# Row maxima of an attention turned and loaded in two parts (in the first batch four), and its score blocks spread over the attention before and its own first steps

## The chip, the cores and the metric

One core of one Trainium2 chip runs the kernel. The metric is the device time of one execution in microseconds; the median of three is given.

## The reference

A transformer block with conditioning, on 8 batches of 512 tokens with 256 features, 16 heads of 16 features. Cut to what matters:

```
c6 = silu(c) @ Wc + bc                         # six shifts, scales and gates per batch
xm = ln(x) * (1 + sc_msa) + sh_msa
q, k, v = xm @ Wq + bq, xm @ Wk + bk, xm @ Wv + bv     # (8, 512, 16 heads, 16)
w = softmax(einsum('bqhc,bkhc->bhqk', q / 16, k))
y = einsum('bhqk,bkhc->bqhc', w, v)
x = x + g_msa * (y @ Wo + bo)
h = gelu((ln(x) * (1 + sc_mlp) + sh_mlp) @ W1 + b1)
x = x + g_mlp * (h @ W2 + b2)
```

## The kernel before

The softmax subtracts the true row maximum, so the scores are computed twice. A **score block** is one matmul (line 598): 128 queries of one head against its 512 keys, into one of two score banks (6 and 7). DVE takes its row maximum into `mx` (`row_max`, line 899). There are 16 heads x 4 query tiles = 64 blocks a batch. A block may be issued once the block two before it has had its maximum taken (`max_done`).

When the maxima are there, TensorE **turns** them (`turn_maxima`, line 608: transposes of `mx` into a bank), DVE writes them as two bf16 rows per head, a high and a low part (`maxima_rows`, lines 922 and 924, into `mrow`), and SP loads these into rows 96 and 97 of the q stack (`load_maxima`, line 294). The k stack has -1 there, so that the second, **transposed scores** (line 628, 98 rows) come out with the maximum subtracted, and ACT applies the exponential (line 500). The q and k stacks themselves hold the parts of q and k, and are filled by four large loads a batch, from a DRAM scratch (line 322).

The work is a pipeline written out by hand. `step(i)` holds, in this order: the attention of batch i (sixteen steps `s`; in each the transposed scores of four heads for one key tile in two pairs, then the product with V of the step before, `pv`, line 620); the turning of the normalised x of batch i+2 and of batch i-1; q, k and v of batch i+2; the MLP of batch i-1 (`up` and `down` products for j = 0 to 7); the output projection of batch i (`wo_products`), in whose middle stand the first transposed scores of batch i+1 (`first_transposed`); and at last DVE's `residual` of batch i (lines 1014 and 1017). Steps 2 to 5 are a loop; the others are written out, and in steps -2 and -1 (`early`) there is no attention. The score blocks of batch i+1 are strewn through `step(i)`: `C_BLOCKS` says how many in each step of the attention, `TURN_BLOCKS`, `QK_BLOCKS`, `V_BLOCKS`, `UP_BLOCKS`, `DOWN_BLOCKS` how many at the places after it. In an attention step, `between` puts the first block behind the first pair of transposed scores, the second behind the second pair, the others behind `pv`.

Each engine runs its own list in order. Batch 0 is different already: only the blocks of heads 0 to 7 and eight more are done before its attention, the other 24 stand in its first six steps (`OLD_BLOCKS`), and their maxima are turned after step 5 and awaited at step 8.

DVE also has the layer norms inside the attention, in pieces (`ln2`, `ln1`: 0 to 3 statistics, 4 the variance, 5 to 8 the normalisation of a tile).

Of the kernel before, what the change touches and what calls it, by code (L numbers as in the profile page):

```python
# [53 lines left out]
assert sum(map(sum, (C_BLOCKS, TURN_BLOCKS, QK_BLOCKS, V_BLOCKS, UP_BLOCKS, DOWN_BLOCKS))) == NH * TT  # L54
# [6 lines left out]
assert HALF + EXTRA + sum(OLD_BLOCKS) == NH * TT and OLD_TURN < STEPS // 2  # L61
# [6 lines left out]
def dit_block(nc, x, c, Wc, bc, Wq, bq, Wk, bk, Wv, bv, Wo, bo, W1, b1, W2, b2, out,  # L68
              c6_scr, parts_scr, y_scr, r_scr):
    with ExitStack() as ctx:  # L70
# [97 lines left out]
        half_turned, half_rows, half_loaded = sem("half_turned"), sem("half_rows"), sem("half_loaded")  # L168
# [65 lines left out]

        def c_blocks(i, s):

            return (OLD_BLOCKS[s], NEW_BLOCKS[s]) if isinstance(i, int) and i == 0 else (0, C_BLOCKS[s])

        def tail_blocks(i):

            new = NEW_BLOCKS if isinstance(i, int) and i == 0 else C_BLOCKS
            return NH * TT - sum(map(sum, (new, TURN_BLOCKS, QK_BLOCKS, V_BLOCKS)))
# [8 lines left out]
        def _(sp):  # L251
# [24 lines left out]
            def step(i, par):  # L276
# [14 lines left out]
                def load_maxima(stack, first, last, loaded):  # L291

                    for n in range(2):
                        sp.dma_start(stack[MROW + n:MROW + n + 1, first:last, :], mrow[0:last - first, n, :]).then_inc(loaded, 16)

                if runs(i, 0) and not later(i, 0, 1):
                    sp.wait_ge(mrow_done, 2)
                    load_maxima(qst[par], NH // 2, NH, m_loaded)
                if runs(i, 0):


                    for g in range(NG):
# [50 lines left out]
                if early(i) and runs(i, 1):  # L353
                    sp.wait_ge(half_rows, 2)
                    load_maxima(qst[1 - par], 0, NH // 2, half_loaded)
                elif runs(i, 1):
                    sp.wait_ge(mrow_done, 2 * i + 4)
                    load_maxima(qst[1 - par], 0, NH, m_loaded)
# [189 lines left out]
        def _(pe):  # L548
# [36 lines left out]
            def scores(i, par, blocks, banks=(6, 7)):  # L585

                for _ in range(blocks if runs(i, 1) else 0):
# [7 lines left out]
                    if n == 0:  # L595
                        if later(i, 1, 1):
                            pe.wait_ge(mrow_done, 2 * (i + 1))
# [3 lines left out]
            def turn_maxima(i, first=0, last=NH, turned=mt_done, bank=6):  # L601

                if runs(i, 1):
                    pe.wait_ge(max_done, 64 * (i + 1) + TT * last)
                    if bank == 4:
                        pe.wait_ge(vaug_done, 4)
                    for t in range(TT):
                        m = pe.transpose(ps[0:last - first, bank, t * P:(t + 1) * P], mx[:, t, first:last], ident[:])
                    m.then_inc(turned, 1)
# [22 lines left out]
            def first_transposed(b, par):  # L632

                if later(b, 0, 1):
                    pe.wait_ge(m_loaded, 32 * (b + 1))
                else:
                    pe.wait_ge(half_loaded, 32)
                pe.wait_ge(part_l, 4 * (b + 2) if runs(b, 1) else 4 * NB)
                if later(b, 0, 2):
                    pe.wait_ge(o_gated, b - 1)  # L640
                for p in range(2):
                    transposed_scores(b, par, 0, p)

            def step(i, par):
                has_b, has_c, has_a, has_mlp = runs(i, 1), runs(i, 0), runs(i, 2), runs(i, -1)
                others = (lambda n: 0) if early(i) else (lambda n: n)
                if has_c:
# [4 lines left out]
                    for s in range(STEPS):  # L652
# [7 lines left out]
                        if s == STEPS // 2 and not later(i, 0, 1):  # L660
                            pe.wait_ge(m_loaded, 32)
                        for p in range(2):
# [3 lines left out]
                            if later(i, 0, 1):  # L666
# [6 lines left out]
                        if s == OLD_TURN and not later(i, 0, 1):  # L673
                            turn_maxima(i - 1, NH // 2, NH)
# [66 lines left out]
                if has_mlp:  # L741
# [51 lines left out]
                elif early(i):  # L793
                    scores(i, par, HALF + 2, (6, 7, 0, 1))
                    turn_maxima(i, 0, NH // 2, half_turned, 4)
                    scores(i, par, EXTRA - 2)
                else:
                    scores(i, par, tail_blocks(i))
                    turn_maxima(i)
# [10 lines left out]
        def _(dve):  # L810
# [77 lines left out]
            def row_max(i, blocks, banks=(6, 7)):  # L888
# [3 lines left out]
                for _ in range(blocks):  # L892
                    n = block_at[0]
                    block_at[0] = (n + 1) % (NH * TT)
                    if n == 0 and later(i, 1, 1):
                        dve.wait_ge(mt_done, i + 1)
# [13 lines left out]
            def maxima_rows(i, heads=NH, turned=mt_done, done=mrow_done, bank=6):  # L910

                if not runs(i, 1):
                    return
                if turned is mt_done:
                    dve.wait_ge(mt_done, i + 2)
                    if later(i, 1, 1):
                        dve.wait_ge(m_loaded, 32 * (i + 1))
                    else:
                        dve.wait_ge(half_loaded, 32)
                else:  # L920
                    dve.wait_ge(turned, 1)
                dve.tensor_copy(mrow[0:heads, 0, :], ps[0:heads, bank, :]).then_inc(done, 1)
                dve.wait_ge(done, 2 * (i + 1) + 1)
                dve.tensor_tensor(mrow[0:heads, 1, :], ps[0:heads, bank, :], mrow[0:heads, 0, :], ALU.subtract).then_inc(done, 1)

            def step(i, par):
# [3 lines left out]
                ln2 = {2: (0, 1), 3: (2, 3), 4: (4,), 7: (5, 6), 8: (7, 8)}  # L930
                ln1 = {5: (0, 1), 6: (2, 3), 9: (4,), 12: (5, 6), 13: (7, 8)}
                for s in range(STEPS):
# [13 lines left out]
                    if s == OLD_TURN and has_c and not later(i, 0, 1):  # L946
                        maxima_rows(i - 1, NH // 2)
# [71 lines left out]
                if has_mlp:  # L1019
                    b = i - 1  # L1020
                    row_max(i, UP_BLOCKS[0])
                    for j in range(JT):
# [10 lines left out]
                        if j == JT - 1:  # L1033
                            maxima_rows(i)
# [21 lines left out]
                else:  # L1056
                    if early(i):
                        row_max(i, HALF + 2, (6, 7, 0, 1))
                        maxima_rows(i, NH // 2, half_turned, half_rows, 4)
                        row_max(i, EXTRA - 2)  # L1060
                    else:
                        row_max(i, tail_blocks(i))
                        maxima_rows(i)
# [39 lines left out]
```

## Time and profile before

| | |
|---|---|
| median of three runs | 781.13 us (777.75 to 783.33) |
| the profiled execution | 775.7 us, span 773.8 us |
| TensorE, matmuls | 707.6 us, 91% of the span |
| DVE | 582.3 us, 75% |
| ACT | 384.3 us, 50% |
| GpSimd | 222.3 us, 29% |
| row maxima on DVE (line 899) | 512, 335.4 us, 685 ns each |
| score blocks on TensorE (line 598) | 512 |
| exponentials on ACT (line 500) | 256, 247.9 us, 1022 ns each |
| mean granted clock of TensorE | 0.951 of full speed |

Busy matmul time is modelled and rows overlap, so 91% doesn't say that TensorE runs at its peak. Times within the run are microseconds from the start of the span.

### The profile page before, as it was taken

To read this page: it belongs to the slowest core of one execution; us is meant where nothing else is said; L and a number is where in the kernel's file an instruction comes from. 1 tells how busy PE (TensorE), PEld (TensorE's weight loads), DVE (VectorE), ACT (ScalarE), POOL (GpSimd) and SP (SyncE) were. 2 spreads that over 40 slices of the span, in tenths; PEclk is the share of its full clock that TensorE was granted. 3 is DMA by queue.
4 is the path that set the end of the run, shared out by engine and by line. 5 is a ranking of instruction groups with operands and counts; after the bars stand their busy time and mean duration, and the time that the engine had idled before them with its cause. 6 is when DMAs were issued, how large, how long until landed. Compare 5 with 4: busy or idle time off the path is not lost.

```text
span 773.8 us, 11775 instructions
## 1 busy us (share of the span) xinstructions
PE 707.6 (91%) x3967; PEld 382.9 (49%) x3967; DVE 582.3 (75%) x1015; ACT 384.3 (50%) x462; POOL 222.3 (29%) x163
## 2 busy tenths in 40 slices
PE   4678989769999999999999899999999998998986
PEld 1551222432268425772378225862478225812976
DVE  5769688859886898789887798789886976721463
ACT  0430556217752676347642775257633773298221
POOL 5245001200334031511253032512162022230444
PEclk9785799959999999999999999999999999999998
DMA  8489100681039302860067303840076102021110
GB/s 290 138 253 289 62 21 22 223 203 55 28 136 261 99 28 73 257 165 34 31 218 176 112 15 121 247 141 28 30 243 166 59 27 72 3 82 45 56 35 27
DMA packets 59558, 88.45 MB, mean 114 GB/s; under 512 B 6214, under 2 KB 47708, under 8 KB 56428
## 3 DMA queue, kind: packets, MB, share of 16 engines
q1 hardware_dynamic: 59500, 87.69, 37.0%
q8 instruction: 35, 0.57, 0.3%
q14 instruction: 23, 0.19, 0.1%
HBM read 49.35 MB, written 38.06 MB: 113 GB/s over the span
## 4 chain that ended last, share of the span: by engine, by line
issue 34%; PE 32%; DVE 14%; POOL 11%; DMA 5%; ACT 3%; SPq 1%; POOLq 0%; DVEq 0%; ACTq 0%
DVE mx L899 7%; PE ps L620 7%; PE ps L598 7%; PE ps L628 6%; PE ps L552 5%; POOL hl L445 4%; PE ps L759 3%; POOL prob L438 2%; PE ps L763 2%; DMA qst<-mrow 2%; ACT prob L500 1%; DMA kst<-parts_scratch 1%; POOL x L418 1%; POOL xd L431 1%; POOL zl L397 1%
## 5 line engine op out<-in xcount | busy, mean ns | idle before, releaser
L899 DVE TENSOR_REDUCE mx<-ps 128x1 f32<-128x512 f32 x512 | 335.4, 685 | 62.6 <-PE ps L598 56.4
L500 ACT ACTIVATE prob<-ps 128x1024 f32<-128x1024 f32 x256 | 247.9, 1022 | 156.5 <-PE ps L628 156.2
L598 PE MATMUL ps<-kst,qst 96*128 96x512 bf16 x512 | 196.2, 405 | 24.9 <-DVE mx L899 19.0
L628 PE MATMUL ps<-qst,kst 98*128 98x512 bf16 x512 | 150.4, 385 | 4.0 <-DMA qst<-mrow 2.4
L598 PEld LDWEIGHTS ps<-kst,qst 96*128 96x128 bf16 x512 | 45.5, 98 | 191.5 <-DVE mx L899 165.8
L620 PE MATMUL ps<-prob,vaug 128*32 128x512 f32 x1024 | 137.6, 609 | 0.5 <-ACT prob L500 0.3
L445 POOL TENSOR_TENSOR hl<-z,hh 128x512 fp32r<-128x512 f32 x64 | 82.3, 1287 | 137.3 <-DVE hh L1028 137.3
L539 ACT ACTIVATE z<-ps,bias_t 128x512 f32<-128x512 f32 x64 | 44.1, 689 | 134.5 <-PE ps L763 127.1
L393 POOL TENSOR_TENSOR rstd<-vare,mhalf 128x4 f32<-128x4 f32 x16 | 16.4, 1022 | 249.6 <-DVE vare L839 249.6
L628 PEld LDWEIGHTS ps<-qst,kst 98*128 98x128 bf16 x512 | 46.9, 99 | 70.1 <-ACT prob L500 26.6
L438 POOL TENSOR_TENSOR prob<-prob 128x512 bf16<-128x512 f32 x32 | 37.4, 1167 | 139.7 <-DVE prob L973 139.7
L552 PE MATMUL ps<-w_hi,hh 128*128 128x256 f32 x256 | 73.6, 288 | 0.3 <-POOL hl L445 0.3
L552 PE MATMUL ps<-w_hi,hl 128*128 128x256 f32 x256 | 72.0, 281 | 0.0
L552 PE MATMUL ps<-w_lo,hh 128*128 128x256 f32 x256 | 71.9, 281 | 0.0
L1028 DVE CAST hh<-z 128x512 fp32r<-128x512 f32 x64 | 37.0, 580 | 35.8 <-ACT z L539 35.8
L759 PE MATMUL ps<-zh,w_hi 128*128 128x512 f32 x128 | 60.5, 472 | 2.0 <-DVE zh L904 2.0
L759 PE MATMUL ps<-zh,w_lo 128*128 128x512 f32 x128 | 51.5, 402 | 0.0
L552 PEld LDWEIGHTS ps<-w_hi,hh 128*128 128x128 f32 x256 | 48.2, 188 | 2.9 <-POOL hl L445 0.7
L552 PEld LDWEIGHTS ps<-w_lo,hh 128*128 128x128 f32 x256 | 48.2, 188 | 1.8
L552 PEld LDWEIGHTS ps<-w_hi,hl 128*128 128x128 f32 x256 | 48.2, 188 | 0.0
L620 PEld LDWEIGHTS ps<-prob,vaug 128*32 128x32 f32 x1024 | 20.4, 108 | 46.1 <-issue 41.9
L478 ACT ACTIVATE z<-ps,mod 128x512 f32<-128x512 f32 x30 | 21.7, 774 | 39.9 <-DVE bias_t L883 18.5
(106 smaller groups left out, 854.4 us busy)
## 6 DMA issues: line engine op xcount, KB each, us to landing
parts_scratch<-prob SPq DMA_DIRECT2D x32, 384.0 KB, 2.9
qst<-parts_scratch SPq DMA_DIRECT2D x16, 768.0 KB, 9.1
kst<-parts_scratch SPq DMA_DIRECT2D x16, 768.0 KB, 14.0
parts_scratch<-prob SPq DMA_DIRECT2D x32, 256.0 KB, 3.1
y_scratch<-rb SPq DMA_DIRECT2D x32, 256.0 KB, 2.0
xa<-in_x_dram SPq DMA_DIRECT2D x8, 512.0 KB, 4.4
parts_scratch<-prob SPq DMA_DIRECT2D x32, 128.0 KB, 2.9
xd<-in_x_dram SPq DMA_DIRECT2D x8, 512.0 KB, 3.5
```

The lines of the kernel that those rows point to most:

```text
L438: pool.tensor_tensor(parts[:, j, PART_AT[j // 2][2], :], rest[:, j % 2, :], parts[:, j, 1, :], ALU.subtract).then_inc(part_l, 1)
L445: pool.tensor_tensor(hl[:, j % HR, :], hb[:, j % HB, :], hh[:, j % HR, :].bitcast(F32), ALU.subtract).then_inc(hl_done, 1)
L478: act.activation(z_of(n, b)[:, k, :], ps[:, banks + k, :], ACT.Identity, bias=mod[:, 2 * shift + k, bass.ds(b, 1)], scale=mod[:, 2 * scale ...
L500: act.activation(prob[:, s % 2, 2 * p:2 * p + 2, :], ps[:, 2 * p:2 * p + 2, :], ACT.Exp, scale=1.0 / DH).then_inc(exp_done, 1)
L539: act.activation(hb[:, j % HB, :], ps[:, 4 + j % 2, :], ACT.Gelu, bias=b1_t[:, j:j + 1]).then_inc(gelu_done, 1)
L552: m = pe.matmul(out_, a, b, start=start and n == 0, stop=stop and n == 2, skip_group_check=True)
L598: pe.matmul(ps[:, banks[n % len(banks)], :], qst[1 - par][0:MROW, h, t * P:(t + 1) * P], kst[1 - par][0:MROW, h, :], start=True, stop=True ...
L620: m = pe.matmul(ps[32 * q:32 * q + 32, 4 + g % 2, :], vaug[par][:, kt, G * g + q, :], prob[:, s % 2, q, :], start=kt == 0, stop=kt == TT - ...
L628: m = pe.matmul(ps[:, q, :], kst[par][0:KROWS, G * g + q, kt * P:(kt + 1) * P], qst[par][0:KROWS, G * g + q, :], start=True, stop=True)
L759: pe.matmul(ps[:, 4 + j % 2, :], w1[n][:, k, f], zh_of(1, b)[:, k, :], start=k == 0 and n == 0, stop=False)
L899: dve.tensor_reduce(mx[:, t, h:h + 1], ps[:, banks[n % len(banks)], :], AXX, ALU.max).then_inc(max_done, 1)
L1028: dve.tensor_copy(hh[:, j % HR, :], hb[:, j % HB, :]).then_inc(hh_done, 1)
```

## The change

Every batch now does what batch 0 did, and batch 0 does it by quarters. Before an attention 40 of its 64 blocks are done (batch 0: 24); the others stand in its first six steps, four in each (batch 0: ten steps), and the blocks of the next batch only behind them: two in each of steps 6 to 14, three in step 15 (batch 0: four in each of steps 10 to 15). The maxima of heads 0 to 7 are turned after the first `down` product of the MLP in place of the sixth, those of heads 8 to 15 after step 5 of the attention itself, and awaited at step 8. In batch 0 heads 0 to 3 are turned before the attention, the others after steps 1, 5 and 9, and awaited at steps 4, 8 and 12. The 19 blocks outside the attention are dealt out otherwise: `UP_BLOCKS` 5 in place of 3, `DOWN_BLOCKS` 8 in place of 10. The layer norm's pieces move to later steps. The semaphores of the halves fall away; `mt_done`, `mrow_done` and `m_loaded` now count turns.

```
-C_BLOCKS = (1, 0) + (3,) * (STEPS - 4) + (4, 4)
+HALF, EXTRA = NH * TT // 2, 8
+QUARTER = NH * TT // 4
+OLD_BLOCKS = (4,) * 6 + (0,) * (STEPS - 6)
+NEW_BLOCKS = (0,) * 6 + (2,) * (STEPS - 7) + (3,)
 TURN_BLOCKS, QK_BLOCKS, V_BLOCKS = (1, 1), (0, 1, 0, 1), (0, 1, 0, 1)
-UP_BLOCKS, DOWN_BLOCKS = (1, 1, 1), (2, 2, 2, 2, 2, 0, 0, 0)
-HALF, EXTRA = NH * TT // 2, 8
-OLD_BLOCKS = (4,) * 6 + (0,) * (STEPS - 6)
-NEW_BLOCKS = (0,) * 6 + (4,) * (STEPS - 6)
-OLD_TURN = 5
+UP_BLOCKS, DOWN_BLOCKS = (1, 2, 2), (0, 0, 2, 2, 2, 2, 0, 0)
+DOWN_TURN = 0
+FIRST_OLD = (4,) * 10 + (0,) * (STEPS - 10)
+FIRST_NEW = (0,) * 10 + (4,) * (STEPS - 10)
+TURNS, FIRST_TURNS = {5: 8}, {1: 4, 5: 8, 9: 12}
...
+        def heads_of(b, head):
+            return head + (NH // 4 if first(b) else NH // 2)
+        def turn_no(b, head):
+            return head // 4 + 1 if first(b) else 2 * b + 3 + head // 8
...
                     for g in range(NG):
                         sp.wait_ge(y_evac, NG * i + g + 1)
                         sp.dma_start(y_scr[...], ysb[:, g % 2, :]).then_inc(y_written[g % 2], 16)
+                        if g == 0:
+                            load_maxima(i, qst[par], 8)
+                        if g == 1 and first(i):
+                            load_maxima(i, qst[par], 12)
...
+                    if t == 0 and h in (8, 12) and first(i + 1):
+                        pe.wait_ge(mrow_done, 2 * turn_no(i + 1, h - 4))
+                    elif t == 0 and h == 8:
+                        pe.wait_ge(mrow_done, 2 * turn_no(i + 1, 0))
+                    elif n == 0 and later(i, 1, 1):
+                        pe.wait_ge(mrow_done, 2 * (turn_no(i + 1, 0) - 1))
...
-                        if s == STEPS // 2 and not later(i, 0, 1):
-                            pe.wait_ge(m_loaded, 32)
+                        if s == STEPS // 2 or s and s % TT == 0 and first(i):
+                            pe.wait_ge(m_loaded, 32 * turn_no(i, s))
...
-                        if s == OLD_TURN and not later(i, 0, 1):
-                            turn_maxima(i - 1, NH // 2, NH)
+                        if s in c_turns(i):
+                            turn_maxima(i, c_turns(i)[s])
...
-                        if j == 5:
-                            turn_maxima(i)
+                        if j == DOWN_TURN:
+                            turn_maxima(i + 1, 0)
...
-                    scores(i, par, HALF + 2, (6, 7, 0, 1))
-                    turn_maxima(i, 0, NH // 2, half_turned, 4)
+                    scores(i, par, QUARTER + 2, (6, 7, 0, 1))
+                    turn_maxima(i + 1, 0, 4)
                     scores(i, par, EXTRA - 2)
...
-                ln2 = {2: (0, 1), 3: (2, 3), 4: (4,), 7: (5, 6), 8: (7, 8)}
-                ln1 = {5: (0, 1), 6: (2, 3), 9: (4,), 12: (5, 6), 13: (7, 8)}
+                ln2 = {5: (0, 1), 6: (2, 3), 7: (4,), 9: (5, 6), 10: (7, 8)}
+                ln1 = {7: (0,), 8: (1, 2), 9: (3,), 10: (4,), 12: (5, 6), 13: (7, 8)}
...
-                        if j == JT - 1:
-                            maxima_rows(i)
+                        if j == DOWN_TURN + 2:
+                            maxima_rows(i + 1, 0)
```

## Rows read from the trace of the kernel before

**Rows 1.** windows of batch 5's attention and of the stage after it

```profile
512.20:554.00 41.80, 41.53 (x239) 12.72 (x239) 37.27 (x75) 32.49 (x35) 8.16 (x6) 1.00 0.20 64
554.00:597.00 43.00, 41.11 (x256) 33.82 (x254) 34.26 (x52) 15.48 (x23) 17.27 (x13) 1.00 0.61 180
```

**Rows 2.** table of waits, TensorE: us, times, longest

```profile
PE ps L628 <- DMA qst<-mrow: 2.4, 3, 1.9
```

**Rows 3.** timeline, TensorE, a step with three blocks: start, us, instruction

```profile
539.90 0.39 PE L598 MATMUL ps<-kst,qst 96*128 96x512 bf16 x1
540.13 0.60 PE L628 MATMUL ps<-qst,kst 98*128 98x512 bf16 x2
...
542.75 0.60 PE L628 MATMUL ps<-qst,kst 98*128 98x512 bf16 x2
```

**Rows 4.** timeline, TensorE, batch 7, steps without blocks

```profile
679.75 1.04 PE L628 MATMUL ps<-qst,kst 98*128 98x512 bf16 x4
...
696.56 1.04 PE L628 MATMUL ps<-qst,kst 98*128 98x512 bf16 x4
```

**Rows 5.** timeline, batch 0, a step with four blocks

```profile
93.58 2.58 DVE L899 TENSOR_REDUCE mx<-ps 128x1 f32<-128x512 f32 x4 [0.51 <-PE ps L598]
93.59 1.03 PE L628 MATMUL ps<-qst,kst 98*128 98x512 bf16 x4
...
96.68 1.03 PE L628 MATMUL ps<-qst,kst 98*128 98x512 bf16 x4
```

**Rows 6.** timeline, the seam before batch 5, and the end of its attention

```profile
512.15 1.04 PE L628 MATMUL ps<-qst,kst 98*128 98x512 bf16 x4
...
513.98 0.39 PE L598 MATMUL ps<-kst,qst 96*128 96x512 bf16 x1
...
514.20 1.27 PE L628 MATMUL ps<-qst,kst 98*128 98x512 bf16 x4
...
515.43 1.22 DVE L1017 TENSOR_TENSOR x<-x,xd 128x1024 f32<-128x1024 f32 x1
...
516.57 1.52 DVE L899 TENSOR_REDUCE mx<-ps 128x1 f32<-128x512 f32 x2
...
553.97 1.04 PE L580 MATMUL ps<-ident,xa 128*128 128x128 f32 x8
```

**Rows 7.** timeline, batch 0, the turn after step 5

```profile
98.57 0.42 DVE L828 BATCH_NORM_STATS2 stats<-xa 128x6 f32<-128x256 f32 x1
...
101.60 1.03 PE L628 MATMUL ps<-qst,kst 98*128 98x512 bf16 x4
...
102.51 0.68 DVE L924 TENSOR_TENSOR mrow<-ps,mrow 8x512 bf16<-8x512 f32 x1
...
105.72 1.03 PE L628 MATMUL ps<-qst,kst 98*128 98x512 bf16 x4
```

**Rows 8.** chain that ended last, before batch 0: start, us, what

```profile
53.18 20.42 DVE mx L899 x34
...
74.93 0.78 SPq L294
...
75.75 1.81 DMA qst<-mrow
...
78.32 1.86 PE ps L628 x4
```

**Rows 9.** DMA issues from 65.2 to 65.3: KB, us to landing

```profile
kst<-parts_scratch SPq DMA_DIRECT2D x1, 768.0 KB, 12.7
```

**Rows 10.** chain, then timeline, before batch 1

```profile
163.41 7.20 DMA qst<-mrow
...
170.65 1.04 PE L628 MATMUL ps<-qst,kst 98*128 98x512 bf16 x4 [1.87 <-DMA qst<-mrow]
```

**Rows 11.** windows, PEclk the granted clock

```profile
646.70:650.10 3.40, 3.40 (x10) 2.31 (x9) 1.60 (x4) 0.69 (x1) 0.39 (x1) 0.50 0.29 90
425.60:429.90 4.30, 2.13 (x13) 1.52 (x14) 2.62 (x3) 1.94 (x2) 0.00 (x0) 1.00 0.71 228
```

More of the change, by code:

```diff
@@ L233, in x1_of, with first, c_turns @@
             return xa if final(b) else x1
+        def first(b):
+            return isinstance(b, int) and b == 0
         def c_blocks(i, s):
[L237 to L242, printed above, removed]
+            return (FIRST_OLD[s], FIRST_NEW[s]) if first(i) else (OLD_BLOCKS[s], NEW_BLOCKS[s])
+        def c_turns(i):
+            return FIRST_TURNS if first(i) else TURNS
+        def heads_of(b, head):
+            return head + (NH // 4 if first(b) else NH // 2)
+        def turn_no(b, head):
+            return head // 4 + 1 if first(b) else 2 * b + 3 + head // 8
         def early(i):
@@ L289, in step, with load_maxima @@
                     sp.dma_start(gm[:], c6_scr[bass.ds(i - 1, 1), G2 * H:(G2 + 1) * H].broadcast_to([P, H])).then_inc(gm_loaded, 16)
-                def load_maxima(stack, first, last, loaded):
+                def load_maxima(b, stack, head):
+                    last = heads_of(b, head)
+                    sp.wait_ge(mrow_done, 2 * turn_no(b, head))
                     for n in range(2):
[L294 to L298, printed above, removed]
+                        sp.dma_start(stack[MROW + n:MROW + n + 1, head:last, :], mrow[0:last - head, n, :]).then_inc(m_loaded, 16)
                 if runs(i, 0):
+                    if first(i):
+                        load_maxima(i, qst[par], 4)
                     for g in range(NG):
@@ L352, in step @@
                     load_stack(i + 2, 1, 1)
[L353 to L358, printed above, removed]
+                if runs(i, 1):
+                    load_maxima(i + 1, qst[1 - par], 0)
                 if runs(i, -1):
@@ L594, in scores, with turn_maxima @@
                         pe.wait_ge(stack_loaded[h // 8], 32 * (i + 2))
[L595 to L597 removed]
+                    if t == 0 and h in (8, 12) and first(i + 1):
[4 more added lines that the diff above has]
+                        pe.wait_ge(mrow_done, 2 * (turn_no(i + 1, 0) - 1))
                     pe.matmul(ps[:, banks[n % len(banks)], :], qst[1 - par][0:MROW, h, t * P:(t + 1) * P], kst[1 - par][0:MROW, h, :],
                               start=True, stop=True).then_inc(s_done, 1)
[L601 to L604 removed]
+            def turn_maxima(b, head, bank=6):
+                if runs(b, 0):
+                    last = heads_of(b, head)
+                    pe.wait_ge(max_done, 64 * b + TT * last)
                     if bank == 4:
@@ L607, in turn_maxima @@
                     for t in range(TT):
-                        m = pe.transpose(ps[0:last - first, bank, t * P:(t + 1) * P], mx[:, t, first:last], ident[:])
-                    m.then_inc(turned, 1)
+                        m = pe.transpose(ps[0:last - head, bank, t * P:(t + 1) * P], mx[:, t, head:last], ident[:])
+                    m.then_inc(mt_done, 1)
             def pv(b, par, s):
@@ L665, in step @@
                                 transposed_scores(i, par, s, p)
-                            if later(i, 0, 1):
+                            if not first(i):
                                 between(p, p + 1)
@@ L908, in z_lo, with maxima_rows @@
                 dve.tensor_tensor(zl_of(n, b)[:], z_of(n, b)[:], zh_of(n, b)[:].bitcast(F32), ALU.subtract).then_inc(zl_done[n], 1)
-            def maxima_rows(i, heads=NH, turned=mt_done, done=mrow_done, bank=6):
-                if not runs(i, 1):
+            def maxima_rows(b, head, bank=6):
+                if not runs(b, 0):
                     return
[L914 to L924, printed above, removed]
+                heads, turn = heads_of(b, head) - head, turn_no(b, head)
+                dve.wait_ge(mt_done, turn)
+                if not first(b) or head:
+                    dve.wait_ge(m_loaded, 32 * (turn - 1))
+                dve.tensor_copy(mrow[0:heads, 0, :], ps[0:heads, bank, :]).then_inc(mrow_done, 1)
+                dve.wait_ge(mrow_done, 2 * (turn - 1) + 1)
+                dve.tensor_tensor(mrow[0:heads, 1, :], ps[0:heads, bank, :], mrow[0:heads, 0, :], ALU.subtract).then_inc(mrow_done, 1)
             def step(i, par):
@@ L945, in step @@
                                     norm_piece(0, i + 2, xa, k)
-                    if s == OLD_TURN and has_c and not later(i, 0, 1):
-                        maxima_rows(i - 1, NH // 2)
+                    if has_c and s in c_turns(i):
+                        maxima_rows(i, c_turns(i)[s])
                 row_max(i, others(TURN_BLOCKS[0]))
```

27 lines of the change are left out of this document (13 added, 14 removed).

## The prediction

> **What bounds the kernel now.** I began with the page's busy times, in the table above: TensorE's matmuls fill 91% of the span. The windows of one loop iteration then split it in two. The attention, 512.2 to 554.0, has TensorE busy for 41.53 of 41.80 us, with DVE at 37.27 and ACT at 32.49; the projections and the MLP, 554.0 to 597.0, have it busy for 41.11 of 43.00 [rows 1]. So in the loop TensorE's own queue sets the end, and a change that makes TensorE wait costs its full length. The table of waits says how much the wait for the maxima rows (the one that a half-sized load could shorten) costs now: 2.4 us in three places over the whole run, 1.9 of it in one [rows 2].
>
> The timeline gives a price per attention step. A step has 4 transposed scores, 8 matmuls with V and some score blocks. With three blocks it lasts 542.75 - 540.13 = 2.62 us, and one block delays the next matmul by 540.13 - 539.90 = 0.23 [rows 3]. With no blocks, in the last batch, eight steps take 696.56 - 679.75 = 16.81, so 2.10 each [rows 4]: there ACT's two exponentials set the pace. With four blocks, in the first batch, a step takes 96.68 - 93.59 = 3.09, more than 2.62 + 0.23 = 2.85, and the DVE row says why: four maxima take 2.58 and then DVE is idle 0.51 for the next block [rows 5]. There are only two score banks, so blocks must wait for maxima and maxima for blocks. Four blocks are over the knee, three are not.
>
> **The change in the loop (batches 1 to 6).** The number of blocks inside an attention stays 45 (before 1, 0, twelve times 3, 4, 4; after six times 4, nine times 2, 3), and outside it stays 19. Nothing is saved there; what changes is the order.
>
> - Step 0 has four blocks in place of one. In the trace, DVE does the two residual operations at this seam (lines 1014 and 1017), the second from 515.43 for 1.22 us, and only then its first maximum, at 516.57 (ends overlap the next start a little); the only block of this step was issued at 513.98, long before, and step 1 could begin at 514.20 [rows 6]. After the change blocks 1 and 2 fill both banks at about 514.0 and 514.2; block 3 needs the first maximum, 516.57 + 0.65 = 517.2, block 4 the second, 517.9, and step 1 starts at about 518.2. So step 0 lasts 518.2 - 512.15 = 6.05 in place of 2.05: +4.0. Queued behind the waiting block are all of step 1's transposed scores, and behind them ACT. This is the largest term.
> - Step 1: the V matmuls of step 0 waited for the residual before (it had no block); they no longer do, but it has four blocks. I walk the two-bank handshake through it and get 2.8.
> - Steps 2 to 4: four blocks, 3.09 each, 9.27.
> - Step 5: four blocks and the turn of heads 8 to 15. The first batch did just this: step 5 ran 96.68 to 101.60, 4.92 [rows 5, 7]; TensorE waits for the last maximum, then turns. DVE also did two statistics there, 0.42 each, and will again [rows 7].
> - Step 6: in the first batch 101.60 to 105.72, 4.12, because the next block uses the bank that DVE reads until 102.51 + 0.68 = 103.19 [rows 7]. After, it has two blocks, the first placed between the two pairs of transposed scores. It holds the second pair until about 1.6 after the start; then 0.23 + 0.43 + 0.23 + 1.0 follow. 3.6.
> - Steps 7 to 14: two blocks. No row shows such a step. Bounds: 2.10 (ACT's pace, none) and 2.62 (three). As TensorE is full at three, I take one block off: 2.62 - 0.22 = 2.40; 19.2 for eight.
> - Step 15: three blocks, 2.62.
>
> Sum: 6.05 + 2.8 + 9.27 + 4.92 + 3.6 + 19.2 + 2.62 = 48.5. Before, the same attention ran from 512.15 to 553.97 [rows 6], 41.8. That is +6.6 each, +40 for six. The load of the turned rows is off the path here: the rows are ready 1.6 after step 6 begins, the two issues are 0.8 apart and the second took 1.81 to land before batch 0 [rows 8], some 4.3 in all, and step 8 begins 6.0 after step 6. The norm pieces that move from steps 2 to 8 to steps 5 to 10 go at nothing: steps 7 to 10 have two blocks, so DVE has about 1 us free in each; should that cover go, each piece costs 0.4.
>
> **The last attention (batch 7)** had no blocks and gets 24. Step 0 +4.0, step 1 2.8 - 2.10 = +0.7, steps 2 to 4 3 x 0.99 = +3.0, step 5 4.92 - 2.10 = +2.8; steps 6 and 7 stay at 2.10, so step 8 may find the rows not yet landed, +0.3. Together +10.8.
>
> **The first attention (batch 0)** has 64 blocks as before, in sixteen steps of four, but turns three times instead of once. The turn at step 5 cost 4.92 - 3.09 = 1.8 and 4.12 - 3.09 = 1.0 more, 2.8 in all, some 0.8 of it the statistics on DVE. Two more without these are 2 x 2.0 = 4.0. The turn after step 1 falls where the granted clock is 0.50, +0.5. So +4.5, bounds 2 and 7.
>
> **The two places where blocks are saved.** Before batch 0 sixteen blocks fewer stand ahead of the turn. DVE did the 34 in 20.42 us, 0.60 each, so the rows would be ready 9.6 us earlier than the load at 74.93, at about 65.3 [rows 8]. But this load follows four stack loads of 768 KB in the same queue; the last, issued at 65.2, took 12.7 us to land, so until 77.9 [rows 9]; the rows landed at 75.75 + 1.81 = 77.56 and the first transposed scores began at 78.32 [rows 8]. The new rows' load, a smaller one, would sit behind the same loads and land no earlier than about 77.5. That a small load sits behind the stack loads is shown at the end of the next stage: ready to go at 163.41, it took 7.20 to land, and TensorE, which had sat idle 1.87 for it, went on at 170.65 [rows 10]. So 9.6 us of work are taken from a chain that ends just level with another, and I take a gain of 78.32 - 77.5 = 0.8; likewise 0.3 for the eight blocks fewer in the stage before batch 1. The trace's bounds for both are 0 and 9.6 + 8 x 0.6 = 14.4. In the Trainium skill, "DMA: Bandwidth & Descriptors", section "Queues, rings and completion order", each DMA engine consumes descriptors in ring order, but a DMA on fewer engines may complete before an earlier one on all of them. The trace agrees: 77.56 is 0.3 before the last stack load's end. By that rule a load of four heads on few engines could land somewhat earlier still, and the sum would fall by perhaps another microsecond; each engine still has its share of the stack loads ahead of it.
>
> **The MLP stage.** The turn comes after the first down product instead of the sixth, with the same four transposes and the same two DVE operations; the up products have two more blocks, the down products two fewer. TensorE may wait a few tenths for the last maximum; the wait for the rows at the seam (2.4 less the 1.9 above, so 0.5) goes. I count -0.3 for the whole run.
>
> **Sum** on the profiled execution: 775.7 + 40 + 10.8 + 4.5 - 0.8 - 0.3 - 0.3 = 829.6. The profiled execution is 5.4 under the median of the runs, 781.1, so I add 54 to the median: 835.
>
> **The rivals.**
>
> 1. *The seam wait is hidden* (15%). If DVE could take the first maxima between the residual operations, or ACT's backlog of exponentials covered TensorE's wait, the seven times 4.0 would go: 835 - 28 = 807. Against: DVE runs in order, and the first maximum stands after the second operation in the rows [rows 6], and a step 0 that lasts 6.05 is longer than the four exponentials ACT has in hand (2.10 a pair, by its pace in the last batch).
> 2. *The clock falls* (15%). TensorE's granted clock is 0.50, the lower of its levels 1.2 and 2.4 GHz, for 3.4 us from 646.70, after a stretch with little matmul work. Against: at 425.6 to 429.9 it was busy for 2.13 of 4.30 and kept 1.00 [rows 11]. The new seam has about 2.4 of 6.05. If it fell there in each attention, 3.4 us would run at half speed: +1.7, seven times, 12: 847. The Trainium skill, "TensorE: Matmul & The Clock Gate", section "Part 1: The HAM clock gate", says that idleness takes the clock to the lower level and activity releases it; the rows agree in kind and leave the seam open.
> 3. *Faster* (5%). The stages before batch 0 and before batch 1 are worth their 14.4, the blocks cost TensorE the same wherever they stand, and the last attention pays only six steps at 2.85 - 2.10, 4.5. Then 781 - 14.4 + 4.5 = 771. It needs the small loads to overtake the stack loads (for it: they begin to move while those are in flight) and both handshake and turn to cost nothing, and it decides if the first transposed scores start before 75.
> 4. *No difference* (4%): the same neutrality in the loop, with the loads in order: 781 + 4.5, within 1%. A per cent is about what a measurement of this kernel can tell from no change.
>
> The forecast has 60%; 1% is left for more than 855. The range takes in the first two rivals and the unknown costs. With two-block steps at 2.62 the six attentions cost 11 more, 846; with them at 2.10 and four-block steps at 2.85, 20 less, 815. So 806 to 853.
>
> **What would show it.** In the changed trace: first transposed scores at 78 and batch 1's at about 174 or 175 (its stage unchanged, the attention before it longer); each loop attention near 48.5; at each seam one pause of TensorE of some 3 us ahead of a score block, released by a maximum; DVE nearly idle from 68 to 78; far more waits of score blocks for maxima; two-block steps at 2.40. The prediction is wrong if the loads overtake, if step 1 starts within 3 us of the first transposed scores, or if the two-block steps run at ACT's pace.

## The result and the profile after

The changed kernel takes 858.42 us (854.82 to 858.74, four runs) against 780.52 us for the kernel before (777.75 to 783.33, four runs): ratio 1.0985, 95% interval 1.0958 to 1.1012. Slower as forecast, but by 78 us and not by 54; it lies 5 us above the range. The profiled execution has a span of 855.8 us, so 82 more than before.

The page of the changed kernel: the span, the engines (busy us, share, instructions) and the granted clock in 40 slices.

```profile
span 855.8 us, 11928 instructions
...
PE 735.5 (86%) x4003; PEld 388.7 (45%) x4003; DVE 592.8 (69%) x1033; ACT 386.0 (45%) x462; POOL 222.2 (26%) x163
...
PEclk9785999669999899999999899997999999989999
```

The same clock row of the kernel before:

```profile
PEclk9785799959999999999999999999999999999998
```

TensorE's share falls from the 91% of the table above to 86% although it has 28 us more busy time, and the clock row, nines throughout the loop in the kernel before, now has eights and a seven there; the mean granted clock fell from 0.951 to 0.920. (A matmul counts as busy for longer at the lower clock, so part of those 28 us is the clock itself.)

The seam ahead of batch 5, in the timeline (start, us, instruction, idle before it and its releaser); the rows of before are [rows 6].

```profile
561.79 1.04 PE L649 MATMUL ps<-qst,kst 98*128 98x512 bf16 x4
...
563.62 0.61 PE L618 MATMUL ps<-kst,qst 96*128 96x512 bf16 x2
...
565.08 1.22 DVE L1032 TENSOR_TENSOR x<-x,xd 128x1024 f32<-128x1024 f32 x1
566.22 3.76 DVE L918 TENSOR_REDUCE mx<-ps 128x1 f32<-128x512 f32 x6
...
566.96 0.39 PE L618 MATMUL ps<-kst,qst 96*128 96x512 bf16 x1 [2.73 <-DVE mx L918]
...
567.78 0.60 PE L649 MATMUL ps<-qst,kst 98*128 98x512 bf16 x2
...
570.62 0.60 PE L649 MATMUL ps<-qst,kst 98*128 98x512 bf16 x2
```

The first two score blocks go out at 563.62, DVE finishes the residual at 566.30, and block 3 follows its first maximum at 566.96, after TensorE has been idle for 2.73. From the first transposed scores to step 1 it is 567.78 - 561.79 = 5.99; the forecast was 6.05. Step 1 lasts 570.62 - 567.78 = 2.84 (forecast 2.8).

The turn after step 5 of the same attention, TensorE alone; before, batch 0 had it [rows 7].

```profile
584.53 0.60 PE L629 MATMUL ps<-ident,mx 128*8 128x128 f32 x4 [1.17 <-DVE mx L918]
584.97 0.60 PE L649 MATMUL ps<-qst,kst 98*128 98x512 bf16 x2
586.71 0.61 PE L618 MATMUL ps<-kst,qst 96*128 96x512 bf16 x1 [1.15 <-DVE mrow L939]
587.11 1.06 PE L649 MATMUL ps<-qst,kst 98*128 98x512 bf16 x2
...
590.40 1.03 PE L649 MATMUL ps<-qst,kst 98*128 98x512 bf16 x2
...
594.94 1.03 PE L649 MATMUL ps<-qst,kst 98*128 98x512 bf16 x2
```

The turn waits 1.17 for the last maximum, and the first new block 1.15 for the rows. Then the pairs of transposed scores change from 0.60 to 1.06, the step from 584.97 to 590.40 lasts 5.43 where I had 3.6, and the next 4.54 where I had 2.40. The windows of this attention, of the stage behind it, and of the stretch that begins with those long matmuls show why (us, busy time by engine, then the granted clock, DMA share and GB/s).

```profile
561.79:615.38 53.59, 47.79 (x244) 13.64 (x242) 39.79 (x77) 32.68 (x35) 8.18 (x6) 0.90 0.15 50
615.38:657.98 42.60, 40.91 (x255) 33.87 (x256) 32.17 (x51) 15.47 (x23) 17.26 (x13) 1.00 0.62 182
586.40:596.60 10.20, 9.89 (x30) 2.21 (x31) 4.58 (x15) 3.88 (x5) 1.02 (x1) 0.50 0.01 3
```

For 10.2 us the granted clock is 0.50, the lower of the two levels, 1.2 GHz, with TensorE busy for 9.89 of them: it had idled at the two places just before. The attention takes 53.6 in place of 41.8 [rows 6]; the stage behind it 42.6 against 43.0 [rows 1].

Before batch 0, SP's issues (start, us, then what), and the chain that ended last:

```profile
63.46 0.89 SPq L343 DMA_DIRECT2D qst<-parts_scratch  x2
64.45 2.05 SPq L343 DMA_DIRECT2D kst<-parts_scratch  x2
66.64 1.35 SPq L314 DMA_DIRECT2D qst<-mrow  x2
```

```profile
69.92 9.96 issue
79.88 1.87 PE ps L649 x4
```

The rows' load goes out at 66.64, 8 us earlier than before [rows 8], but behind the four stack loads, and the first transposed scores begin at 79.88, not earlier at all. The chain calls the 9.96 us up to them "issue", which means that this profile shows no releaser for them; that they are the load's is shown by experiment 4. Before batch 1 the chain names the load:

```profile
163.67 15.05 DMA qst<-mrow
...
178.77 1.89 PE ps L649 x4
```

The load takes 15.05 to land, where it took 7.20 [rows 10], and TensorE sits idle 6.17 for it, where it was 1.87. It is issued 24 us after the attention's last transposed scores (138.4) in place of 32 (131.2), so what it gained in readiness it lost in the queue.

### The profile page after: what moved, and what is told of

Read it like the earlier page. It is cut to its first block, busy times and chain, and to the rows that moved or that the text cites. A ratio compares the mean times of both kernels' runs of the same rounds, so it can differ in the third digit from the quotient of the medians.

```text
span 855.8 us, 11928 instructions
## 1 busy us (share of the span) xinstructions
PE 735.5 (86%) x4003; PEld 388.7 (45%) x4003; DVE 592.8 (69%) x1033; ACT 386.0 (45%) x462; POOL 222.2 (26%) x163
## 4 chain that ended last, share of the span: by engine, by line
PE 58%; DVE 17%; issue 14%; POOL 6%; ACT 2%; DMA 2%; SPq 1%; DVEq 0%; POOLq 0%; ACTq 0%
PE ps L641 11%; PE ps L618 11%; PE ps L569 10%; PE ps L649 9%; DVE mx L918 8%; PE ps L777 6%; PE ps L781 3%; DMA qst<-mrow 2%; PE ps L718 2%; PE ps L746 1%; POOL x L435 1%; POOL xd L448 1%; DVE prob L985 1%; PE ps L629 1%; DVE x L1029 1%
## 5 line engine op out<-in xcount | busy, mean ns | idle before, releaser
L618 PE MATMUL ps<-kst,qst 96*128 96x512 bf16 x512 | 193.9, 412 | 55.8 <-DVE mx L918 37.7
L649 PE MATMUL ps<-qst,kst 98*128 98x512 bf16 x512 | 159.7, 404 | 16.8 <-issue 10.0
L641 PE MATMUL ps<-prob,vaug 128*32 128x512 f32 x1024 | 146.6, 646 | 0.3 <-ACT prob L517 0.3
L1043 DVE CAST hh<-z 128x512 fp32r<-128x512 f32 x64 | 31.6, 495 | 41.7 <-ACT z L556 41.7
L781 PE MATMUL ps<-zl,w_hi 128*128 128x512 f32 x128 | 41.3, 404 | 0.1
```

Of the source, the lines that this page charges most:

```text
L618: pe.matmul(ps[:, banks[n % len(banks)], :], qst[1 - par][0:MROW, h, t * P:(t + 1) * P], kst[1 - par][0:MROW, h, :], start=True, stop=True ...
L641: m = pe.matmul(ps[32 * q:32 * q + 32, 4 + g % 2, :], vaug[par][:, kt, G * g + q, :], prob[:, s % 2, q, :], start=kt == 0, stop=kt == TT - ...
L649: m = pe.matmul(ps[:, q, :], kst[par][0:KROWS, G * g + q, kt * P:(kt + 1) * P], qst[par][0:KROWS, G * g + q, :], start=True, stop=True)
L781: m = pe.matmul(ps[:, 4 + j % 2, :], w1[0][:, k, f], zl_of(1, b)[:, k, :], start=False, stop=k == KC - 1)
L1043: dve.tensor_copy(hh[:, j % HR, :], hb[:, j % HB, :]).then_inc(hh_done, 1)
```

## The experiments

Times of the kernel before, on the chips of these runs: 779 to 781 us. The changed kernel was not run again beside them, so that a difference from its 858.42 us also holds what the chips differ by, and four runs of one kernel lie up to 9 us apart (experiment 3). Such differences are good to a few microseconds; the ratios are taken against the kernel before on the same chip.

**1. TensorE kept busy in the waits.** At the seam the first two blocks are computed six times over; after the turn six score matmuls go to the free bank 7. Cut and put into plainer words:

```
-  pe.matmul(ps[:, bank, :], ...).then_inc(s_done, 1)
+  for _ in range(6 if s == 0 and first two blocks and not first(i) else 1):
+      m = pe.matmul(ps[:, bank, :], ...)
+  m.then_inc(s_done, 1)
...
+  if s == 6 and p == 0 and runs(i, 1) and not first(i):      # ahead of the first new block
+      for _ in range(6): pe.matmul(ps[:, 7, :], ...)
```

> The changed kernel with TensorE kept busy in the two waits of batches 1 to 7: at the seam the first two score blocks are computed six times over (the same result, signalled after the last), and after the turn of step 5 six extra score matmuls go to the free bank 7 ahead of the first new block. Neither should end later than the wait that it fills. Theory A (the part of the loss beyond my sum is the clock, which falls in these waits): the granted clock stays 1.00 through the loop's attentions, step 1 lasts 2.84 and step 6 3.7 everywhere as they did in batch 5 and batch 6 of the changed kernel where the clock was full, and the time falls by 15 to 22 us, to about 838 to 843. Theory B (the falls of the clock only accompany longer waits): nothing is gained, 858 or slightly more.

839.93 us (839.24 to 842.51), ratio 1.0801 (1.0767 to 1.0835). Adding 106 matmuls takes 18.5 us away by the medians, 17.3 by the spans of the profiled executions (855.8 and 838.5), and 14 by the ratios (1.0985 and 1.0801, whose intervals lie far apart). Windows of batch 5: the attention, step 0, and the stretch with the turn.

```profile
550.02:599.00 48.98, 46.49 (x260) 14.62 (x259) 39.70 (x78) 32.54 (x35) 8.18 (x6) 1.00 0.17 55
550.02:556.00 5.98, 5.20 (x28) 2.76 (x27) 4.70 (x6) 1.94 (x2) 0.00 (x0) 1.00 0.60 179
571.00:575.00 4.00, 2.83 (x19) 1.28 (x15) 3.05 (x6) 1.44 (x2) 0.00 (x0) 1.00 0.20 70
```

The granted clock is 1.00 in all of it. The timeline of TensorE there, at the seam and after the turn:

```profile
550.02 1.04 PE L653 MATMUL ps<-qst,kst 98*128 98x512 bf16 x4
...
551.85 2.77 PE L619 MATMUL ps<-kst,qst 96*128 96x512 bf16 x12
555.18 0.39 PE L619 MATMUL ps<-kst,qst 96*128 96x512 bf16 x1 [0.57 <-DVE mx L927]
...
556.00 0.60 PE L653 MATMUL ps<-qst,kst 98*128 98x512 bf16 x2
...
558.84 0.60 PE L653 MATMUL ps<-qst,kst 98*128 98x512 bf16 x2
...
573.19 0.60 PE L653 MATMUL ps<-qst,kst 98*128 98x512 bf16 x2
573.62 1.46 PE L692 MATMUL ps<-kst,qst 96*128 96x512 bf16 x6
...
576.90 0.61 PE L653 MATMUL ps<-qst,kst 98*128 98x512 bf16 x2
```

Step 0 is 5.98, step 1 is 2.84 and step 6 is 576.90 - 573.19 = 3.71. In the changed kernel step 1 lasted 2.84 in batch 5 alone, 4.3 to 5.4 in the others, and step 6 from 3.7 to 5.4 in batches 1 to 6; here they are 2.84 in all seven and 3.70 or 3.71 in all six. Theory A holds: step 0 and the turn take as long as they did (5.98 and 4.91), what follows them is at full clock, and the time fell. The Trainium skill, "TensorE: Matmul & The Clock Gate", section "Part 1: The HAM clock gate", says that idleness takes the clock to the lower level and activity releases it. The trace agrees in its two levels, 0.50 and 1.00, and in that filling the pauses kept the upper one.

**2. The order of the blocks alone.** One line of the kernel before:

```
-C_BLOCKS = (1, 0) + (3,) * (STEPS - 4) + (4, 4)
+C_BLOCKS = (4,) * 6 + (2,) * (STEPS - 7) + (3,)
```

> The kernel before with one line changed: the 45 blocks of an attention in the order six times 4, nine times 2, 3, all of them of the next batch. It has the seam wait and the steps above the knee, but neither the turn inside the attention, nor the second load, nor any block in the last attention. Theory A (pattern and seam carry most of the loss): per loop attention 6.0 + 2.8 + 4 x 3.14 + 9 x 2.40 + 2.65 = 45.7 against 41.8, +3.9, and one fall of the clock at the seam, +1.7, for six batches: 780.5 + 33 = 814. Theory B (the turn inside the attention is the cause): within 1% of 780.

816.19 us (812.41 to 818.72), ratio 1.0500 (1.0465 to 1.0535): about half of the whole loss, from one line that adds nothing and removes nothing. In the profiled execution step 0 lasts 6.0 to 6.2 in batches 1 to 3, 5, 6, the four-block steps 3.0 to 3.3, the two-block steps 2.40; step 1 is 2.84 where the clock held (batches 5 and 6) and 4.4 to 5.4 where it fell. The seam ahead of batch 5:

```profile
539.77 1.04 PE L628 MATMUL ps<-qst,kst 98*128 98x512 bf16 x4
...
544.93 0.39 PE L598 MATMUL ps<-kst,qst 96*128 96x512 bf16 x1 [2.73 <-DVE mx L899]
...
545.75 0.60 PE L628 MATMUL ps<-qst,kst 98*128 98x512 bf16 x2
```

It is the seam of the changed kernel, 5.98 long with a pause of 2.73, without any turn in the attention. Theory A holds.

**3. Batch 0 by halves.** `FIRST_OLD, FIRST_NEW = OLD_BLOCKS, NEW_BLOCKS`, one turn after step 5, 40 blocks before the attention; the rest as changed.

> The changed kernel with batch 0 treated by halves like the others: 40 of its 64 blocks before the attention, one turn after step 5, new blocks 2 a step. Theory A (quarters gain nothing at the start, because the rows' load waits behind the stack loads, and cost two turns): the first transposed scores still begin at 78 to 80, the attention of batch 0 is about 8 us shorter (two turns fewer and fewer four-block steps) while the stage behind it gains blocks that the stack loads hide, and the time is 850 to 853. Theory B (quarters do bring the first attention forward): it begins 9 us later and the time is 858 or more.

844.60 us (841.84 to 850.76), ratio 1.0881 (1.0829 to 1.0933): 14 us less than the changed kernel; theory A's direction, twice its size. The first transposed scores begin at 79.6 although 16 more blocks stand ahead of them, so the quarters brought nothing there. The attention of batch 0 lasts 46.5 to its last transposed scores in place of 58.5 (two turns fewer, two-block steps at 2.40 for four-block ones at 3.1), and the stage behind it 40.9 in place of 40.4, so its three blocks more cost little. The attention is 12 shorter, where I had expected 8. About 1.3 of it, by my estimate, is clock: in the changed kernel the two steps at the turn after step 9 last 4.82 and 5.17, 3.6 above two steps of 3.18, with the clock at 0.50 for 3.4 us, and those at the turn after step 5 (4.86 and 3.73) are only 2.3 above 3.09 and 3.18.

**4. The rows' load ahead of the k stack loads**, in the two stages before batches 0 and 1 only:

```
                     load_stack(i + 2, 0, 1)
+                    if isinstance(i, int) and i <= 0 and runs(i, 1):
+                        load_maxima(i + 1, qst[1 - par], 0)
                     ...
                     load_stack(i + 2, 1, 0)
```

> The changed kernel with one order changed on SP, in the two stages before batch 0 and batch 1 only: the load of the turned rows is issued before the two k stack loads of the batch after, not behind them. Theory A (the small load waits for what is ahead of it in the queues): the first transposed scores begin at about 74 in place of 79.9 and those of batch 1 some 11 us earlier than in the changed kernel in all, and the time is 847. Theory B (something else holds the first attention, GpSimd's memset of the k stack or the score blocks): batch 0 still begins at 78 to 80, time 856 to 858.

846.41 us (842.20 to 850.66), ratio 1.0860 (1.0817 to 1.0902): 12 us less by the medians, 11 were expected (7.0 less by the profiled spans). SP's issues and TensorE:

```profile
63.64 0.89 SPq L343 DMA_DIRECT2D qst<-parts_scratch  x2
66.38 1.35 SPq L314 DMA_DIRECT2D qst<-mrow  x2
67.84 0.84 SPq L343 DMA_DIRECT2D kst<-parts_scratch  x2
...
74.00 1.87 PE L651 MATMUL ps<-qst,kst 98*128 98x512 bf16 x4 [4.39 <-issue]
```

The rows' load is issued at nearly the same time as in the changed kernel (66.38, there 66.64), with two stack loads ahead of it and not four, and the first transposed scores begin at 74.00 in place of 79.88. So it was the place in the queue that held them; the score blocks and GpSimd's memset were done by 70. The Trainium skill, "DMA: Bandwidth & Descriptors", section "Queues, rings and completion order", says that each DMA engine takes its descriptors in the order of the ring; the trace agrees, in these 5.9 us. The stage before batch 1 is 33.0 in place of 40.4. Batch 0's attention is 2.5 longer, as more of it lies ahead of the clock's rise (at 90.8 here, at 88.0 there), and batch 1's begins at 167.95 in place of 178.77.

**5. The same blocks, not at the seam.** The changed kernel with

```
-OLD_BLOCKS = (4,) * 6 + (0,) * (STEPS - 6)
+OLD_BLOCKS = (1, 0, 5, 6, 6, 6) + (0,) * (STEPS - 6)
```

> The changed kernel with the 24 late blocks of batches 1 to 7 moved out of the seam: 1, 0, 5, 6, 6, 6 in steps 0 to 5 in place of six times 4. Theory A (from the seam to the turn DVE is the bound: it can't begin before the residual is done, and then needs 24 maxima, so that the place of a block doesn't matter): steps 0 to 5 last 23 us together as in the changed kernel (5.99 + 2.84 + 3 x 3.14 + 4.91 = 23.2), and only the clock's behaviour may move the time; 845 to 860. Theory B (the wait at the seam is a cost of its own, and goes when no block waits there): 4.0 less in seven attentions, about 830.

849.86 us (847.91 to 851.62), ratio 1.0915 (1.0865 to 1.0966). The steps of batch 5's attention, by the transposed scores that begin them, to the turn and the first after it:

```profile
553.58 1.04 PE L649 MATMUL ps<-qst,kst 98*128 98x512 bf16 x4
...
555.63 1.27 PE L649 MATMUL ps<-qst,kst 98*128 98x512 bf16 x4
...
557.97 0.60 PE L649 MATMUL ps<-qst,kst 98*128 98x512 bf16 x2
...
575.92 0.60 PE L629 MATMUL ps<-ident,mx 128*8 128x128 f32 x4 [0.80 <-DVE mx L918]
576.36 0.60 PE L649 MATMUL ps<-qst,kst 98*128 98x512 bf16 x2
```

Step 0 is back at 2.05 and step 1 at 2.34, as before [rows 6], and yet steps 0 to 5 last 576.36 - 553.58 = 22.8 together, against 584.97 - 561.79 = 23.2 in the changed kernel. The 4.0 of the seam are not a cost of their own: from the end of the residual to the turn DVE with its 24 maxima is the bound, wherever they stand. (In the changed kernel DVE is busy for 15.7 of the 18.2 us from 566.3 to 584.5, and idle 0.63 once a step, for the first block behind the products with V; here that gap comes once in six maxima.) Theory A holds. The kernel did gain 8.6 us by the medians (5.5 by the ratios). What differs in the traces is the clock, which no longer falls at the seam but still does after the turn in five of the six loop attentions (step 6 at 5.1 to 5.4, and 3.7 in batch 2).

**6. 48 blocks before an attention.** `DOWN_BLOCKS` 0, 0, 4, 4, 4, 4, 0, 0 and

```
-OLD_BLOCKS = (4,) * 6 + (0,) * (STEPS - 6)
+OLD_BLOCKS = (1, 0, 4, 4, 4, 3) + (0,) * (STEPS - 6)
```

> The changed kernel with 48 of the 64 blocks done before an attention (the eight more in the down products, four each), and 16 late ones as 1, 0, 4, 4, 4, 3. Theory A (DVE is the bound between seam and turn, 0.65 a maximum and some handshake): steps 0 to 5 take eight maxima less, 23.2 - 5.2 - 0.5 = 17.5, the MLP stage grows by 8 x 0.22 = 1.8 as long as DVE keeps up there, so about 3.5 to 4 less in each of seven attentions, and step 1 at full clock more often: 822 to 833. Theory B (the turn and its waits are what costs): within 5 of 858.

838.82 us (834.09 to 840.87), ratio 1.0750 (1.0695 to 1.0805). Windows of batch 5's attention and the stage behind it:

```profile
555.44:599.10 43.66, 41.18 (x236) 12.32 (x235) 34.86 (x70) 32.54 (x35) 8.18 (x6) 1.00 0.19 61
599.10:647.94 48.84, 44.04 (x264) 34.41 (x264) 36.99 (x59) 15.48 (x23) 17.19 (x13) 1.00 0.55 159
```

Steps 0 to 5 last 17.8 (expected 17.5), the attention 43.7, and the clock holds at 1.00. But the stage behind it lasts 48.8, with TensorE idle for 4.8 of it, all of it waiting for maxima, where the changed kernel had 42.6 and idled 1.7: eight more maxima in the down products cost 6.2 there, not 1.8. DVE's maxima are no cheaper to place in the MLP at four a product. That term of the expectation failed, and the time lies above the 822 to 833 of theory A as well as far under theory B. The fair comparison is experiment 1, which has the full clock too: there the loop's period is 91.5 in batch 3 and 91.6 in batch 5, here 92.5 in both. So in the loop the moved blocks gained nothing and cost 1 us a batch; of the 19.6 us against the changed kernel the loop's part is the clock, and the last attention, with eight blocks fewer and no stage to take them, is 5.3 shorter than in experiment 1. The clock held in the attentions of batches 2 to 6 although nothing fills the turn and its pauses are nearly the same (0.79 and 1.15 in batch 5, in the changed kernel 1.17 and 1.15): what decides that a pause costs clock stays open.

**7. Fewer new blocks in batch 0's attention.** One line of the kernel before:

```
-NEW_BLOCKS = (0,) * 6 + (4,) * (STEPS - 6)
+NEW_BLOCKS = (0,) * 6 + (3,) * (STEPS - 6)
```

> The kernel before with one line changed: batch 0's attention takes three new blocks a step in its last ten steps in place of four, and the stage behind it ten more. Theory A (from the run with batch 0 by halves: that stage ends with the stack loads, not with its blocks, so blocks moved into it are hidden and the attention runs under the knee, 2.62 in place of 3.1 a step): batch 1 starts about 3 to 4 us earlier and the time is 3 to 4 us under the kernel before, ratio 0.995 to 0.996. Theory B (the added blocks are on the path there, 0.60 each): no gain, or up to 2 us slower.

777.74 us (775.31 to 780.77, twelve runs), ratio 0.9982 (0.9960 to 1.0005): no gain that can be told. The attention is 4.2 us shorter and the stage behind it 4.9 longer. The chain there:

```profile
163.09 0.70 DVE mx L899
...
163.84 1.04 PE ps L608 x4
164.90 0.69 DVE mrow L922
...
166.22 1.21 DVE yc L994
...
168.56 3.75 PE ps L728 x16
```

It now runs through the last maxima, the turn and the rows to the scaling of y, which DVE does only afterwards, and to the output projection; the load is no longer in it. Theory A's slack was smaller than ten blocks. The granted clock of the stage was lower too, 0.50 from 145.4 to 172.7, where the kernel before had it so from 151.8 to 168.9; what that cost was not tried apart.

**8. The seam's wait filled alone** (experiment 1 without its second edit).

> The changed kernel with TensorE kept busy at the seam only (the first two score blocks of an attention computed six times over), nothing added after the turn. With both waits filled the time was 839.9. Theory A (each wait lets the clock fall for itself): step 1 lasts 2.84 in all attentions, step 6 still 4.7 to 5.4 in some, and the time lies between, 845 to 851. Theory B (it is the seam alone that brings the clock into trouble, the turn follows from it): 840.

850.58 us (844.33 to 853.48), ratio 1.0911 (1.0848 to 1.0974). Step 1 is 2.84 in all seven attentions; step 6 is 4.9 to 5.4 in batches 2 to 6. The window of the fall behind batch 5's turn:

```profile
580.90:587.70 6.80, 6.27 (x18) 1.43 (x18) 3.57 (x12) 2.80 (x4) 0.00 (x0) 0.50 0.02 5
```

So the clock can fall at either wait without the other: here behind the turn, in experiment 2 behind the seam. By the medians the seam's filling is worth 7.8 us and the turn's the other 10.7, by the profiled spans (855.8, 846.9, 838.5) 8.9 and 8.4; with four runs from 844 to 853 the division is no finer than about half each. Theory A holds.

**9 and 10. A place between.** In the kernel before, batch 0's new blocks are 4 in steps 6 to 10 and 3 in steps 11 to 15 (9); and also the rows' load ahead of the k stack loads before batch 1 (10).

```
-NEW_BLOCKS = (0,) * 6 + (4,) * (STEPS - 6)
+NEW_BLOCKS = (0,) * 6 + (4,) * 5 + (3,) * (STEPS - 11)
```

> The kernel before with batch 0's attention at four new blocks in steps 6 to 10 and three in steps 11 to 15 (35 in place of 40), five more behind it. In the run with three everywhere, ten more blocks there outlasted the stack loads: the attention was 4.2 us shorter, the stage behind it 4.9 longer. Theory A (there is slack for some of them, about the difference between rows ready at 162.8 and their landing behind the stack loads at 170.5): batch 1 starts about 2 us earlier than in the kernel before, ratio 0.997. Theory B (no slack): 1.000.

> The same, and in the stage before batch 1 the load of the turned rows is issued before the two k stack loads. Theory A (as the run with this order in the changed kernel showed, the rows' load then lands within some 3 us of its issue): TensorE's wait of 1.9 us ahead of batch 1's first transposed scores goes too, batch 1 starts 3 to 4 us earlier than in the kernel before, ratio 0.995. Theory B (the k stack loads, issued later, are now late for the first score block of batch 2, and hold TensorE in attention 1): the gain is given back, 1.000.

Run 9: 776.77 us (776.65 to 777.33), ratio 0.9941 (0.9921 to 0.9962). Run 10: 777.27 us (775.41 to 782.74), ratio 0.9961 (0.9942 to 0.9980). Both are faster than the kernel before by their intervals, run 9 by more than its theory A (0.997), run 10 by about its own (0.995). But the profiled executions show only 0.3 and 0.5 us of it (from batch 0's first transposed scores to batch 1's it is 92.0 and 91.8, before 92.3), and ahead of batch 1's first transposed scores the wait of 1.9 us on the rows' load is gone in both, in run 9 with the loads in their old order. The spans, 774.9 and 774.0, are no shorter than the 773.8 of the kernel before, whose profiled execution was a fast one of its kind. So I take the edit for a small gain whose size is open; the load's order adds nothing to it that can be told.

## Why the prediction was right and wrong

**Right: what bounds the kernel, and the price of a step.** With the clock held (experiment 1), the steps of a loop attention are 5.98, 2.84, 3.14, 3.14, 3.15, 4.91, 3.71 and 2.40; the prediction had 6.05, 2.8, 3.09, 4.92, 3.6 and 2.40. The two-block step, which no row of before showed, was TensorE's own work, as taken, and neither bound: in seven of them TensorE is busy for all 16.85 us. The first step is longer in batches 1 and 4, 7.59 and 8.54, as it was in the kernel before (2.46 and 4.36); the sum had batch 5's seam for all.

**Right: no gain at the two starts.** The rows' loads waited behind the stack loads, and experiment 4 shows that their place in the queue held the first attention. The 0.8 and 0.3 that I allowed did not come; the profiled start was 1.6 us later instead, which is what the starts of the runs scatter over here (79.1 to 81.3 in those with the same order of loads). Batch 1's first transposed scores, forecast for about 174 or 175, began at 178.77: besides the later start, the attention before them was 5.6 longer and the stage 1.0.

**Wrong: rival 2 was put down as a rival.** The failed step is its "against": that the stretch from 425.6 to 429.9, busy for 2.13 of 4.30, had kept 1.00 [rows 11]. One stretch that kept the clock was weighed more than the one next to it in the same group that had lost it. The stretch ahead of that loss, 640.0 to 646.7, was no emptier, busy for 3.45 of 6.70. And the seam of the "against" doesn't always keep the clock: in the profiled execution of experiment 9, busy for 2.19 of 4.30 from 424.7 to 429.0, it was followed by 3.4 us at 0.50 from 430.3. The clock did fall, and the rival itself was too small: I priced one place per attention at half speed for 3.4 us, seven times 1.7 = 12. In fact there were two places, the seam and the turn, and stretches of 3.4 to 10.2 us; filling both waits is worth 18.5 by the medians (14 by the ratios). With 18.5 in the sum the forecast would have been 835 + 18.5 = 853.5, 5 under the measured median.

**What remains** is best taken between profiled executions. Experiment 1, without the clock's falls in the loop, has a span of 838.5, 64.7 above the kernel before; the sum was 53.9. The 10.8 between: the start (2.0 later, not 0.8 earlier), batch 0's attention (5.5, not 4.5), the stage behind it (1.7 longer, not 0.3 shorter), the loop's six periods (43.1 in all, not 39.7; from 6.6 in batch 3 to 7.7 in batch 6), the last attention and the end (12.4, not 10.8). Five small misses, all of one sign. The first, 2.8, is about what the starts scatter by (78.3 to 81.3); what makes the others was not tried. Between medians less remains, 78 - 54 - 18.5, about 5, because the profiled execution of the kernel before was 4.8 under its median and that of the changed kernel at its own.

**Right for a reason that I had split wrongly:** I called the 4.0 of the seam "the largest term". Experiment 5 shows that the seam is only where the queue of DVE's maxima first shows; taken away there, it comes back in steps 2 to 5. The sum was right, since it priced the steps as they stood, but rival 1 (28 us less without the seam's wait) could never have been had by moving blocks within the six steps. Experiment 6, which takes eight maxima out of them, did shorten them by 5.3, and lost 6.2 in the MLP.

Where the 78 us went, by the experiments: order and number of blocks per step with their clock falls, about 37 (experiment 2); batch 0 by quarters, 14 (experiment 3); what is left, some 27, goes to the seven turns inside the attention, their clock falls and the late blocks of the last attention. The parts overlap in the clock and were not each tried alone, so this last division is worked out and not shown.

## What to carry to other kernels

Price a change of order by the engine that runs next to the bound: here three blocks a step fitted under DVE's rate and four did not, and an equal count dealt out unevenly cost 5%, the wait at the seam and the clock included. A load made ready earlier gains nothing while it is issued behind larger ones; look at what is queued ahead of it before counting the time saved. Waits on TensorE of one to three microseconds inside a busy phase cost the wait here and, in most batches, some microseconds more in clock: when a change adds one, give the fall a term in the sum, or put harmless matmuls into it. And when a variant is faster, compare it with one that has the same clock before you credit its blocks (experiment 6).

## What the runs showed of the hardware

- 106 added matmuls made the kernel 18.5 us faster by the medians (14 by the ratios), because the granted clock stayed at 1.00 in the loop's attentions (batch 5: 5.20 busy of 5.98 at the seam, without them 3.05 of 5.99) in place of falling to 0.50 for up to 10.2 us behind pauses of 2.73 and of 1.17 and 1.15 us.
- The fall isn't the same from batch to batch: with the same instructions, step 1 took 2.84 in batch 5 and 4.3 to 5.4 in the others, step 6 took 3.7 in batches 2 and 6 and up to 5.43 in batch 5. In experiment 6 it took 3.7 in batches 2 to 6, unfilled, behind nearly the same pauses.
- The second of the two small loads of the rows took 1.8 us to land with one stack load nearly done ahead of it (8 KB) [rows 8], 7.2 behind the tail of the stack loads (16 KB) [rows 10] and 15.05 behind all four of them (8 KB).
